# A gated delta layer: token halves of four batches exchanged, triangle solve in opposite corners of the TensorE array, output by channel

## The chip, the cores and the metric

One Trainium2 chip, one of its cores. The metric is the device time of one execution in microseconds (us), the median of several. The kernel is a decoder of 12 sub-layers on 16 batches of 128 tokens and 256 channels, all in float32 at this place; the change touches one sub-layer, the gated delta attention of layer 1 (`layer1_delta`), and two of its constants.

## What is computed

Cut from the reference. Every token has 8 key heads and 16 value heads of 128 channels; `w_qkvz` gives queries, keys, values and the gate z, `w_ba` gives beta and the decay.

```
q, k, v = split(silu(causal_conv4(x @ w_qkvz.T)))
beta = sigmoid(b);  g = -exp(A_log) * softplus(a + dt_bias)
q = q * rsqrt(sum(q * q) + 1e-6);  k = k * rsqrt(sum(k * k) + 1e-6)
def step(S, (qt, kt, vt, gt, bt)):
    S = S * exp(gt)
    delta = (vt - einsum('bhk,bhkv->bhv', kt, S)) * bt
    S = S + einsum('bhk,bhv->bhkv', kt, delta)
    return S, einsum('bhk,bhkv->bhv', qt * 128 ** -0.5, S)
xf = o * silu(z)
xn = xf * rsqrt(mean(xf * xf, -1) + 1e-6) * norm_weight
return xn.reshape(B, T, 16 * 128) @ w_out.T
```

The layer norm of x plus this follows.

## The kernel before

The recurrence over 128 tokens is written as matrices: with A the decayed, beta-weighted, strictly triangular product of keys, the new values are (I + A)^-1 V, and the output is the decayed product of keys and queries times them.

**Rounds.** `layer1_delta` runs 16 rounds. Round i takes key head i // 2 and half of the batches (`batch0(i)`): 8 batches by 2 value heads make 16 slots of 128x128. Everything of a round is in two halves h of 8 slots (`heads(t, h)`); h = 0 is batches 0 to 3, h = 1 batches 4 to 7. Each engine has one function `round_(i)`, an order written out by hand; in it stand the parts of round i, the projections and convolutions of round i + 1 and the gate norm and output projection of round i - 1. Engines meet at semaphores only. PSUM is eight banks, used as four units of two (`unit(n)`).

**TensorE** (`pe`), in order: `turn_values` (L1214, values to token rows), `multiply_keys` (L1220; per batch one product of 256 columns, keys and queries by keys), `project` for round i + 1 (L1200, four units of 1024 columns), `turn_output` of round i - 1 (L1231), `gate_project` (L1208, tokens by channels), `project_out` of i - 1 for h = 0 (L1237), the first triangle product e1 (L1243), `project_out` for h = 1, the sums of squares for the next norm (L1226), three more triangle products (xT1, wT, xT2, L1243: the 64x64 inverses by a Newton step), and the solve. The solve makes the upper 64 rows (`upper`, L1261), takes them across (`across`, L1265), and makes the lower rows (`lower`, L1269), in four quarters of four slots; last the reads, att by solved values (L1388).

**The inverse of the diagonal blocks.** `aT` has 16x16 blocks on its diagonal, 8 for each slot. SyncE sends them to memory, one DMA for each of the 8 block rows with all 16 slots (L1132: 16 partitions by 16 slots by 64 bytes), waits for all, and loads them with one block to each partition (L1134). VectorE inverts all 128 blocks (`invert`, L1672 to L1713, 19 instructions); y and its transpose go to memory (L1136, L1137) and back into `x0` and `xT0`, 8 DMAs each (L1143, L1149). e1 needs `x0`; xT1 needs `xT0` and `p1` (L1767).

**ScalarE** copies projections out (`tap`, L1436 and L1438), does Silu, Exp, Ln, squares and the copies between triangle products; functions of different tables have a table load between them. **VectorE** does normalise (L1633), gate (L1718), the products aT and att with the decay (L1653), the sums over the channels of the squared gated output (L1722) and its scaling (L1726), invert, two decay scans (L1648), convolutions (L1593), the additions to x (L1731), the copies xT2 (L1773) and the additions to the lower values (L1778), and the weighing by beta (L1640). **GpSimd** masks aT to al (L1187).

**Norms through memory.** The key norms are sums over partitions, made by TensorE in four rows. ScalarE takes Ln and Exp, SyncE sends four rows out (`norms_out`, L1105) and one broadcast back to 128 partitions (`norms_in`, L1109). The gate norm is not: it is a VectorE sum over channels, since tokens are on partitions there.

Of the kernel before, what the change touches and what calls it, by code (L numbers as in the profile page):

```python
# [7 lines left out]
F32 = mybir.dt.float32  # L8
# [988 lines left out]
def layer1_delta(nc, g):  # L997
    with Layer(nc, "l1a") as L:
# [4 lines left out]
        outer = L.sb("outer", [128, 128])  # L1003
# [7 lines left out]
        floor = g.mem[:, 8:12, :].rearrange("p a n -> p (a n)")  # L1011
# [3 lines left out]
        e, aT, att, al, vt, z, go, oT, uw = (L.sb(n, [128, VH, 128]) for n in "e aT att al vt z go oT uw".split())  # L1015
# [4 lines left out]
        part = L.sb("part", [128, 64])  # L1020
        x0, xT0, ec, p1, xT1, wT = (L.sb(n, [128, VH, 64]) for n in "x0 xT0 ec p1 xT1 wT".split())
# [4 lines left out]
        ss = L.sb("ss", [128, VH])  # L1026
        rs = L.sb("rs", [128, VH])
# [6 lines left out]
            "z_proj z_out u_made u_out r_made vr_made w_made w_out o_made gated gsq gsum g_ln g_rs g_inverted normed "  # L1034
            "o_turned oT_out out added restored ln_stats ln_mean ln_sqrt ln_out x_turned x_turned_out")
# [11 lines left out]
        def projected(i, u):  # L1047

            return unit(u if i else u % 2)
# [7 lines left out]
        def quarter(n):  # L1057
            return ps[:, 4 + n, :].rearrange("p (k n) -> p k n", n=128)
# [10 lines left out]
        def lows(t, q):  # L1069
            return t[0:64, 4 * q:4 * q + 4, :]  # L1070

        def highs(t, q):
            return t[64:128, 4 * q:4 * q + 4, :]
# [15 lines left out]
        def _(sp):  # L1089
            d = g.dram  # L1090
            for t, name in ((outer, "outer_blocks"), (fold, "fold_ident")):
                sp.dma_start(t[:], d[name]).then_inc(s["rest_loaded"], 16)
            sp.dma_start(floor.rearrange("p (k n) -> p k n", n=S), bc(d["diagonal_floor"], 1, HALF)).then_inc(s["rest_loaded"], 16)
# [16 lines left out]

            norms_out(0)
# [7 lines left out]
            for i in range(ROUNDS):  # L1119
# [46 lines left out]
        def _(pool):  # L1166
# [15 lines left out]
            for i in range(ROUNDS):  # L1182
                for h in range(2):
                    if i:
                        pool.wait_ge(s["r_made"], 4 * i)
# [6 lines left out]
        def _(pe):  # L1192
# [63 lines left out]
            def diagonal(t):  # L1256
                return lambda p0, k: t[p0:p0 + 64, k, p0:p0 + 64]
# [3109 lines left out]
```

## Time and profile before

| what | value |
|---|---|
| runs | 2418.24, 2422.37, 2415.96 us; median 2418.24 |
| profiled execution: span | 2424.5 us (no other time of that execution is given) |
| cores, mean granted TensorE clock | 1, 0.931 |
| TensorE busy | 2112.7 us, 87% of the span |
| VectorE busy | 1856.6 us, 77% |
| ScalarE busy | 1477.2 us, 61% |
| GpSimd busy | 216.2 us, 9% |
| the 16 rounds of the delta layer | about 365 to 1275 us |

Times in the profile are from the first instruction. A float32 product appears as two records, a transpose as one. The duration of a record holds the time through the array; the distance between starts is the rate. Line numbers are those of the kernel printed above.

### The profile page before, as it was taken

What the parts mean: (1) busy time and instruction counts of PE and PEld (TensorE: products, weight loads), DVE (VectorE), ACT (ScalarE), POOL (GpSimd) and SP (SyncE); (2) the same over time, 40 slices, a digit from 0 to 9 for tenths busy, and PEclk for the clock granted to TensorE, in tenths of its full rate; (3) what the DMA queues carried; (4) which work ended last, traced back from release to release, by engine and by line L of the source; (5) the groups of instructions that cost most, each with busy time, mean ns of one, the idle gap of its engine ahead of it and who ended that gap; (6) DMA issues with size and microseconds to landing.
All of it is one profiled execution on the core that took longest, in us unless ns stands there. A gap on an engine that the chain in (4) does not pass through costs nothing. (4 is left out here: it accounts for less than half of the span.)

```text
span 2424.5 us, 42274 instructions
## 1 busy us (share of the span) xinstructions
PE 2112.7 (87%) x16920; PEld 1596.5 (66%) x16920; DVE 1856.6 (77%) x3341; ACT 1477.2 (61%) x2466; POOL 216.2 (9%) x163
## 2 busy tenths in 40 slices
PE   7997447999999999999986589899999996888855
PEld 4666325777777777878774345788888873555633
DVE  4776667888989898889867834478888776678697
ACT  3664255667777777776736631577777775455365
POOL 0000100000100010101100042000000000100313
PEclk8998768999999999999988799999999996999977
DMA  3000012222222221222116355311010000200001
GB/s 159 2 1 12 13 34 53 72 83 57 64 56 66 56 64 54 62 74 80 36 49 212 129 143 176 115 32 57 23 27 6 5 18 1 81 2 1 16 1 35
DMA packets 164785, 135.14 MB, mean 56 GB/s; under 512 B 118512, under 2 KB 145776, under 8 KB 157936
## 3 DMA queue, kind: packets, MB, share of 16 engines
q1 hardware_dynamic: 160752, 126.02, 16.6%
q0 software_dynamic: 3840, 6.43, 1.4%
q8 instruction: 135, 2.21, 0.4%
q14 instruction: 58, 0.48, 0.1%
HBM read 106.42 MB, written 25.98 MB: 55 GB/s over the span
## 5 line engine op out<-in xcount | busy, mean ns | idle before, releaser
L1593 DVE SCALAR_TENSOR_TENSOR ctx_chan<-l1a_raw,l1a_cw,ctx_chan 128x1024 f32<-128x1024 f32 x192 | 232.0, 1279 | 3.5 <-issue 3.5
L1200 PE MATMUL banks<-x_chan,l1a_wp 128*128 128x512 f32 x512 | 225.2, 598 | 4.8 <-ACT l1a_vt L1488 4.8
L1200 PEld LDWEIGHTS banks<-x_chan,l1a_wp 128*128 128x128 f32 x512 | 98.0, 192 | 122.6 <-issue 116.7
L3166 PE MATMUL banks<-x_chan,more_weights_ahead 128*128 128x128 f32 x1024 | 123.6, 275 | 1.2 <-ACT l2a_kT L2693 1.2
L3166 PEld LDWEIGHTS banks<-x_chan,more_weights_ahead 128*128 128x128 f32 x1024 | 121.6, 192 | 3.9 <-ACT l2a_kT L2693 2.0
L1187 POOL TENSOR_TENSOR l1a_al<-l1a_aT,l1a_outer 128x1024 f32<-128x1024 f32 x32 | 75.0, 2364 | 483.2 <-DVE l1a_aT L1653 483.2
L1237 PE MATMUL banks<-l1a_wo,l1a_oT 128*128 128x256 f32 x512 | 117.7, 383 | 0.0
L2706 ACT ACTIVATE l2a_masked<-l2a_masked,l2a_rowmax 128x128 f32<-128x128 f32 x256 | 99.0, 392 | 28.9 <-DVE l2a_rowmax L2919 28.9
L3202 PE MATMUL banks<-l2a_wo,l2a_oT 128*128 128x256 f32 x512 | 114.5, 382 | 0.0
L1208 PE MATMUL banks<-l1a_wz,x_chan 128*128 128x256 f32 x512 | 113.4, 380 | 0.0
L3202 PEld LDWEIGHTS banks<-l2a_wo,l2a_oT 128*128 128x128 f32 x512 | 96.2, 190 | 14.3 <-issue 1.0
L1237 PEld LDWEIGHTS banks<-l1a_wo,l1a_oT 128*128 128x128 f32 x512 | 96.5, 191 | 13.6
L1208 PEld LDWEIGHTS banks<-l1a_wz,x_chan 128*128 128x128 f32 x512 | 96.4, 191 | 12.9 <-issue 0.5
L1436 ACT ACTIVATE l1a_raw<-banks 128x1024 f32<-128x1024 f32 x64 | 65.5, 1024 | 48.8 <-PE banks L1200 48.8
L126 PE MATMUL banks<-ident,x_tok 128*128 128x128 f32 x224 | 43.2, 357 | 40.2 <-ACT x_tok L194 18.4
L3470 ACT ACTIVATE l3a_probsT<-banks 128x512 f32<-128x512 f32 x64 | 38.1, 596 | 59.5 <-PE banks L3636 59.5
L1466 ACT ACTIVATE l1a_oT<-l1a_go 128x1024 f32<-128x1024 f32 x32 | 33.9, 1058 | 64.6 <-DVE l1a_go L1718 64.6
L1778 DVE TENSOR_TENSOR l1a_vt<-banks,l1a_vt 64x512 f32<-64x512 f32 x64 | 44.4, 694 | 37.1 <-PE banks L1265 37.1
L1648 DVE TENSOR_TENSOR_SCAN l1a_e<-ctx_tok 128x1024 f32<-128x1024 f32 x32 | 71.4, 2275 | 1.4 <-DMA ctx_tok<-l1a_rows_mem 1.4
L1438 ACT ACTIVATE ctx_chan<-banks,l1a_cw 128x1024 f32<-128x1024 f32 x64 | 71.0, 1110 | 0.0
L126 PEld LDWEIGHTS banks<-ident,x_tok 128*128 128x128 f32 x224 | 34.3, 185 | 48.7 <-ACT x_tok L194 19.8
L1265 PE MATMUL banks<-l1a_uw,l1a_al 64*64 64x128 f32 x512 | 65.4, 280 | 0.3 <-ACT l1a_uw L1529 0.3
(648 smaller groups left out, 5644.1 us busy)
## 6 DMA issues: line engine op xcount, KB each, us to landing
l1a_sq<-l1a_norm_mem SPq DMA_DIRECT2D x16, 1024.0 KB, 4.7
ctx_tok<-l1a_rows_mem SPq DMA_DIRECT2D x16, 1024.0 KB, 8.1
l1f_wgu<-in_l1f_wgu_dram SPq DMA_DIRECT2D x4, 1408.0 KB, 11.4
moe_sums<-l1x_zero SPq DMA_DIRECT2D x2, 2176.0 KB, 18.3
ctx_chan<-in_ctxT_dram SPq DMA_DIRECT2D x2, 2048.0 KB, 13.8
l1a_wp<-in_l1a_wp_dram SPq DMA_DIRECT2D x8, 512.0 KB, 5.5
l1f_wgu<-moe_sums SPq DMA_DIRECT2D x8, 512.0 KB, 7.5
x_chan<-in_xT_dram SPq DMA_DIRECT2D x4, 512.0 KB, 5.2
```

Of the source, the lines that this page charges most:

```text
L126: mm = nc.tensor.transpose(g.ps[:, n % 2, t * 128:(t + 1) * 128], g.x[:, t0 + t, c * 128:(c + 1) * 128], g.ident[:])
L1187: P.tensor_tensor(heads(al, h), heads(aT, h), bc(outer[:], 1, HALF), ALU.mult).then_inc(s["al_made"], 1)
L1200: mm = MM(projected(i, u)[:, q * 512:(q + 1) * 512], wp[:, c, u * 128:(u + 1) * 128], g.xT[:, c, t0:t0 + 512], start=c == 0, stop=c == 1)
L1208: mm = MM(unit(2 + h)[:, b * 256:(b + 1) * 256], g.xT[:, c, t0:t0 + S], wz[:, c, :], start=c == 0, stop=c == 1)
L1237: mm = MM(unit(h)[:, b * 256:(b + 1) * 256], oT[:, HALF * h + 2 * b + r, :], wo[:, r, :], start=r == 0, stop=r == 1)
L1436: A(raw[:, u, :, CONV - 1:], now, ACT.Copy)
L1438: A(conv[:, u, :], projected(i, u), ACT.Copy, scale=cw[:, c, CONV - 1:]).then_inc(s["tap"], 1)
L1593: V.scalar_tensor_tensor(t, raw[:, u, :, j:j + S], cw[:, c, j:j + 1], t, ALU.mult, ALU.add).then_inc(s["conv_done" if step == 2 else "conv ...
L1648: V.tensor_tensor_scan(heads(e, h).rearrange("p k n -> p (k n)"), rows[:, h * 1024:(h + 1) * 1024], floor, 0.0, ALU.add, ALU.max).then_inc ...
L2706: ins = A(probs[:, k, :], masked[:, k, :], ACT.Exp, bias=rowmax[:, k:k + 1], scale=128 ** -0.5, accum_out=rsum[:, k:k + 1])
L3166: mm = mm_(ps[:, 4 + q % 2, k * 128:(k + 1) * 128], wq[:, c, SHARE * q + k, :], g.xT[:, c, tile(i)], start=c == 0, stop=c == 1)
L3202: mm = mm_(ps[:, 6, 0:D], oT[:, h, :], wo[:, h, :], start=h == 0, stop=h == HEADS - 1)
```

## The change

Half h = 1 (batches 4 to 7) keeps its two 64-token halves exchanged: in `e`, `aT`, `att`, `al` and the values, tokens 0 to 63 stand on partitions 64 to 127 and the rest on 0 to 63. Beta is turned accordingly, the scan has a floor of its own for each half, the mask `outer` too. The solve then works for the two halves in opposite corners of the array at the same time: `early` and `late` values have tiles of their own, all 8 slots of both halves go through each step in two groups of four, and the copies in between take 128 partitions. Keys are multiplied in products of 64 rows by 128 columns (the quarter that is zero is left out) with one increment for both halves. The reads come out by channel, with the two token parts accumulated: early for all tokens, late for the last 64. So the gate is projected by channel, the output transposes and their copies go, `go` is the stationary operand of the output projection, and the gate norm becomes a sum over partitions on TensorE which goes through memory (`widths_through`). Both output projections stand behind e1. The blocks are sent in 16 DMAs. Ln of the next norm moves behind the `wT` copies. One scan moves ahead of the inversion.

```diff
+            def widths_through(i):
+                sp.wait_ge(s["g_rs"], i + 1)
+                for j in range(4):
+                    sp.dma_start(width_mem[j:j + 1, :], widths[32 * j:32 * j + 1, :]).then_inc(s["width_out"], 16)
+                sp.wait_ge(s["width_out"], 64 * i + 64)
+                sp.dma_start(gsq[:].rearrange("p k n -> p (k n)"), width_mem.rearrange("j n -> (j n)").partition_broadcast(128)).then_inc(s["width_in"], 16)
...
-                sp.wait_ge(s["a_made"], 2 * i + 2)
...
-                for b in range(8):
-                    here = slice(BLK * b, BLK * b + BLK)
-                    sp.dma_start(blk_mem[b].rearrange("h r c -> r h c"), aT[here, :, here]).then_inc(s["blk_out"], 16)
-                sp.wait_ge(s["blk_out"], 128 * i + 128)
+                for h in range(2):
+                    sp.wait_ge(s["a_made"], 2 * i + h + 1)
+                    for b in range(8):
+                        here, turn = slice(BLK * b, BLK * b + BLK), (BLK * b + 64 * h) % 128
+                        sp.dma_start(blk_mem[b, HALF * h:HALF * h + HALF].rearrange("h r c -> r h c"),
+                                     aT[here, HALF * h:HALF * h + HALF, turn:turn + BLK]).then_inc(s["blk_out"], 16)
+                sp.wait_ge(s["blk_out"], 256 * i + 256)
                 sp.dma_start(blk[:, 0:BLK * BLK], blk_mem.rearrange("b h r c -> (b h) (r c)")).then_inc(s["blk_in"], 16)
+                if i:
+                    widths_through(i - 1)
...
+            def keys_by(h, b, rows, s0, t0):
+                at = (4 * h + b) * S
+                out = unit(2 + h)[rows, b * 256:(b + 1) * 256].rearrange("p (w n) -> p w n", w=2)[:, :, t0:t0 + 64]
+                return MM(out, conv[:, 0, at + s0:at + s0 + 64], conv[:, 0:2, at + t0:at + t0 + 64], start=True, stop=True)
...
+                for b in range(4):
+                    for t0 in (0, 64):
+                        for h in range(2):
+                            keys_by(h, b, first_rows(h), 0, t0)
+                    keys_by(1, b, second_rows(1), 64, 64)
+                    mm = keys_by(0, b, second_rows(0), 64, 64)
                 mm.then_inc(s["products"], 1)
...
+            def sum_gated():
+                for j in range(4):
+                    mm = MM(ps[32 * j:32 * j + 32, 4, :], g.ones[:, 0:32], gsq[:, 4 * j:4 * j + 4, :], start=True, stop=True)
+                mm.then_inc(s["gsum"], 1)
...
+            def upper(h, k):
+                at = first_rows(h)
+                return MM(pairs(1, k // 4)[at, k % 4, :], xT2[at, HALF * h + k, :], early[at, k, :], start=True, stop=True)
+            def across(h, k):
+                at = first_rows(h)
+                return MM(pairs(0, k // 4)[second_rows(h), k % 4, :], al[at, HALF * h + k, 64:128], solved_early[at, k, :], start=True, stop=True)
+            def read_early(h, k):
+                at = first_rows(h)
+                return MM(slots(2 + h)[:, by_channel(h, k), :], solved_early[at, k, :], att[at, HALF * h + k, :], start=k < 2, stop=False)
+            def read_late(h, k):
+                at = second_rows(h)
+                return MM(slots(2 + h)[:, by_channel(h, k), 64:128], solved_late[at, k, :], att[at, HALF * h + k, 64:128], start=False, stop=k >= HALF - 2)
...
             def solve(i):
+                pe.wait_ge(s["xT2_out"], 2 * i + 2)
+                for c in range(2):
+                    each(upper, c).then_inc(s["u_made"], 1)
+                if i:
+                    pe.wait_ge(s["added"], 2 * i)
+                for c in range(2):
+                    pe.wait_ge(s["u_out"], 2 * i + c + 1)
+                    each(across, c).then_inc(s["r_made"], 1)
+                if i + 1 < ROUNDS:
+                    pe.wait_ge(s["norm_ln"], i + 2)
+                for c in range(2):
+                    each(read_early, c)
+                for c in range(2):
+                    pe.wait_ge(s["vr_made"], 2 * i + c + 1)
+                    each(lower, c).then_inc(s["w_made"], 1)
+                for c in range(2):
+                    pe.wait_ge(s["w_out"], 2 * i + c + 1)
+                    mm = each(read_late, c)
+                mm.then_inc(s["o_made"], 1)
```

ScalarE's and VectorE's orders, cut to the moved parts (ScalarE first):

```diff
+                    A(early[first_rows(h), :, :], slots(h)[0:64], ACT.Silu)
+                    A(late[second_rows(h), :, :], slots(h)[64:128], ACT.Silu).then_inc(s["v_out"], 1)
...
+                if i:
+                    width_ln(i - 1)
+                    width_rs(i - 1)
...
-                    norm_ln(i + 1)
...
                 if more:
+                    norm_ln(i + 1)
                     norm_rs(i + 1)
...
                 for h in range(2):
                     take_products(i, h, att, 1).then_inc(s["att_made"], 1)
-                if i:
-                    for h in range(2):
-                        scale_gated(i - 1, h)
+                if more:
+                    scan(i + 1, 0)
                 invert(i)
+                if i:
+                    v.wait_ge(s["width_in"], 16 * i)
+                    for h in range(2):
+                        V.tensor_tensor(heads(go, h), heads(go, h), heads(gsq, h), ALU.mult).then_inc(s["normed"], 1)
                 if more:
-                    for h in range(2):
-                        scan(i + 1, h)
+                    scan(i + 1, 1)
```

## Rows read from the trace of the kernel before

**Rows 1.** The page, its first line.

```profile
span 2424.5 us, 42274 instructions
```

**Rows 2.** Busy time by stretch: us, then busy us (instructions) of each engine, clock, DMA share, GB/s.

```profile
430.00:1210.00 780.00, 777.26 (x7577) 609.37 (x7576) 692.74 (x792) 553.57 (x636) 77.65 (x35) 1.00 0.22 62
```

**Rows 3.** Timeline of TensorE, one round: start, us, engine, line, operation, out<-in, xcount.

```profile
706.55 3.84 PE L1388 MATMUL banks<-l1a_uw,l1a_att 128*128 128x128 f32 x32
710.22 1.91 PE L1214 MATMUL banks<-ident,ctx_chan 128*128 128x128 f32 x16
711.97 3.62 PE L1220 MATMUL banks<-ctx_chan 128*128 128x256 f32 x16
715.42 13.90 PE L1200 MATMUL banks<-x_chan,l1a_wp 128*128 128x512 f32 x32
729.16 1.91 PE L1231 MATMUL banks<-ident,l1a_go 128*128 128x128 f32 x16
730.90 7.07 PE L1208 MATMUL banks<-l1a_wz,x_chan 128*128 128x256 f32 x32
737.81 3.62 PE L1237 MATMUL banks<-l1a_wo,l1a_oT 128*128 128x256 f32 x16
741.36 2.08 PE L1243 MATMUL banks<-l1a_x,l1a_al 64*64 64x64 f32 x64
743.37 3.72 PE L1237 MATMUL banks<-l1a_wo,l1a_oT 128*128 128x256 f32 x16
747.65 1.06 PE L1226 MATMUL banks<-l1a_sq,ones 128*32 128x512 f32 x8 [0.56 <-ACT l1a_sq L1448]
...
754.41 1.96 PE L1261 MATMUL banks<-l1a_vt,l1a_p 64*64 64x128 f32 x16
...
760.08 1.96 PE L1269 MATMUL banks<-l1a_vt,l1a_p 64*64 64x128 f32 x16
761.97 3.28 PE L1388 MATMUL banks<-l1a_uw,l1a_att 128*128 128x128 f32 x27
```

**Rows 4.** Timeline of VectorE in that round.

```profile
710.17 2.36 DVE L1718 TENSOR_TENSOR l1a_go<-banks,l1a_z 128x1024 f32<-128x1024 f32 x2
...
725.33 0.18 DVE L1672 COPY l1a_y<-l1a_blk 128x8 f32<-128x8 f32 x1 [1.70 <-DMA l1a_blk<-l1a_blk_mem]
...
732.12 4.46 DVE L1648 TENSOR_TENSOR_SCAN l1a_e<-ctx_tok 128x1024 f32<-128x1024 f32 x2
736.50 9.63 DVE L1593 SCALAR_TENSOR_TENSOR ctx_chan<-l1a_raw,l1a_cw,ctx_chan 128x1024 f32<-128x1024 f32 x8
...
747.18 1.21 DVE L1767 TENSOR_TENSOR l1a_p<-l1a_ec,l1a_fold 128x1024 f32<-128x1024 f32 x1
```

**Rows 5.** Timeline of ScalarE in that round.

```profile
753.34 1.28 ACT L1462 ACT_TABLE_LOAD   x1
754.64 0.63 ACT L1462 ACTIVATE l1a_lengths<-l1a_lengths 128x512 f32<-128x512 f32 x1
```

**Rows 6.** Timeline of SyncE's queue, and one line of the page's DMA issues.

```profile
716.88 3.77 SPq L1132 DMA_DIRECT2D l1a_blk_mem<-l1a_aT  x8
723.33 0.34 SPq L1134 DMA_DIRECT2D l1a_blk<-l1a_blk_mem  x1
...
733.97 3.75 SPq L1143 DMA_DIRECT2D l1a_x<-l1a_yT_mem  x8
...
757.32 0.34 SPq L1109 DMA_DIRECT2D l1a_sq<-l1a_norm_mem  x1
...
2062.66 0.43 SPq L3438 DMA_DIRECT2D ctx_chan<-l3x_keys_ahead  x1
2063.14 0.44 SPq L3439 DMA_DIRECT2D ctx_tok<-l3x_vals_ahead  x1
...
l1a_sq<-l1a_norm_mem SPq DMA_DIRECT2D x16, 1024.0 KB, 4.7
```

**Rows 7.** Last round: a stretch of the table, and TensorE's timeline.

```profile
1217.00:1221.00 4.00, 3.27 (x16) 3.28 (x17) 3.56 (x12) 1.03 (x1) 0.00 (x0) 0.50 0.13 37
...
1217.73 3.67 PE L1231 MATMUL banks<-ident,l1a_go 128*128 128x128 f32 x16 [6.96 <-DVE l1a_go L1726]
```

**Rows 8.** Timeline of TensorE in the first layer: tiles of 32 rows.

```profile
106.45 1.17 PE L516 MATMUL banks<-l0a_kT,l0a_qT 32*128 32x128 f32 x32
```

More of the change, by code:

```diff
@@ L1014, in layer1_delta @@
         lengths = L.sb("lengths", [128, 512])
-        e, aT, att, al, vt, z, go, oT, uw = (L.sb(n, [128, VH, 128]) for n in "e aT att al vt z go oT uw".split())
+        e, aT, att, al, z, go, gsq = (L.sb(n, [128, VH, 128]) for n in "e aT att al z go gsq".split())
+        early, late, solved_early, solved_late = (L.sb(n, [128, HALF, 128]) for n in "early late solved_early solved_late".split())
         blk = L.sb("blk", [128, PITCH])
@@ new lines, in each @@
+            def each(product, c):
+                for k in range(4 * c, 4 * c + 4):
+                    for h in range(2):
+                        mm = product(h, k)
+                return mm
+            def solve(i):
+                pe.wait_ge(s["xT2_out"], 2 * i + 2)
+                for c in range(2):
[16 more added lines that the diff above has]
+                mm.then_inc(s["o_made"], 1)
@@ L1316, in round_ @@
+                multiply_keys()
                 if more:
@@ L1373, in round_ @@
                 for h in range(2):
-                    slot_half(6, h, within(p1), within(xT0)).then_inc(s["xT1_made"], 1)
+                    slot_half(2, h, within(p1), within(xT0)).then_inc(s["xT1_made"], 1)
+                if i and more:
+                    pe.wait_ge(s["squared"], i + 2)
+                    pe.wait_ge(s["added"], 2 * i - 1)
+                    sum_squares()
                 for h in range(2):
@@ L1380, in round_ @@
                     pe.wait_ge(s["wT_out"], 2 * i + h + 1)
-                    slot_half(6, h, within(ec), within(wT)).then_inc(s["xT2_made"], 1)
+                    slot_half(2, h, within(ec), within(wT)).then_inc(s["xT2_made"], 1)
                 if i == 0:
-                    next_sums()
+                    pe.wait_ge(s["squared"], 2)
+                    sum_squares()
                 solve(i)
-                for h in range(2):
-                    pe.wait_ge(s["w_out"], 4 * i + 2 * h + 2)
-                    for k in range(HALF * h, HALF * h + HALF):
-                        mm = MM(slots(2 + h)[:, k % HALF, :], att[:, k, :], uw[:, k, :], start=True, stop=True)
-                    mm.then_inc(s["o_made"], 1)
             for c in range(DC):
@@ L1494, in round_ @@
                         tap(i + 1, u)
+                if i:
+                    width_ln(i - 1)
+                    width_rs(i - 1)
+                if more:
                     for u in range(2, 4):
                         tap(i + 1, u)
-                if i:
-                    for h in range(2):
-                        output_turned(i - 1, h)
-                if more:
                     for h in range(2):
```

313 lines of the change are left out of this document (128 added, 185 removed).

## The prediction

> **What bounds the kernel now.** The page first: one core, span 2424.5 us [rows 1]. That is 6.3 us above the median of the three runs (2418.24); the sum below is a difference inside the profiled execution and is then laid on the median. Only the delta layer changes. The table of stretches shows that in its 14 full rounds TensorE is busy for 777.26 of 780 us at a granted clock of 1.00 [rows 2]. The same read starts at 706.55 and 761.97 [rows 3]: a round takes 55.42 us. The timeline of TensorE [rows 3] is one unbroken list; those of VectorE, ScalarE and SyncE [rows 4 to 6] show what runs beside it. So TensorE's work bounds the round. What the reader is to see next is how little slack the chain beside it has. From the value transposes at 710.22, which I call zero: both halves of `aT` are made when SyncE starts the eight DMAs of the diagonal blocks, at 6.66; it waits, and issues the load back at 13.11; the inversion starts at 15.11; the eight `x0` loads start at 23.75, take about 3.3 us to the last one's start and, at the 2.0 us that the block load needed from issue to use, are in at 29.05 [rows 4, 6]. The first triangle product starts at 31.14 [rows 3]. The slack is 2.1 us.
>
> **TensorE's list.** Each number is a distance between starts in rows 3. The output transposes go (729.16 to 730.90: 1.74). The keys took 3.45; they become 24 products of 128 columns, 48 records, in two column halves. The nearest rate is that of two 64-wide tiles at once: the 5.67 us from 754.41 to 760.08 hold 16 lone records (at the rate of the last 16, 1.89) and 64 paired ones, so 0.060 each, 2.9 in all. Sums of the gated squares come in: 1.0, as the sums at 747.65. Gate and output projections keep their columns. The solve was 5.67 + 1.89 + 3.67 = 11.23; now it is five passes of 32 paired records, 160 x 0.060 = 9.6, and 0.3 of waits for copies. In pure work that is -1.74 - 0.55 + 1.0 - 1.3, about 2.6 us less a round.
>
> No row has a float32 product on 64 rows and 128 columns. Bounds for the 64 records of the two reads: 32-row tiles of that width ran 32 records in 1.17 us, 0.036 each [rows 8]; one tile at a time costs the 0.115 of the old read. I take 0.060, nearer to the first because those are also row tiles with 128 columns; the ends are -1.5 and +3.5 us a round. For the keys the upper end is likewise 0.115 a record, +2.7.
>
> Changes of tile shape rise from 5 to 13 a round. At 741.36 and 743.37 [rows 3] the next shape starts 0.07 us before the modelled end of the last record, where equal shapes, as at 711.97, overlap by 0.16: a change costs about 0.1. Three or four are on the new path; I take 0.3. The Trainium skill, TensorEngine Tiling (Array Packing), Key Properties, says that changing the tiling mode drains TensorE. A full drain would be some 0.2 a change and speaks against this change of the kernel; the trace shows the smaller price.
>
> **New waits.** (a) `o_made` now comes once, after the last read, so both gates start behind it (at 710.17 they overlapped it [rows 4]). The norm of the next keys is later too. Its Ln no longer runs ahead of the triangle products but after the `wT` copies, before the Exp: the Exp with its table load takes 1.94 [rows 5], and I count the Ln the same. The trip through memory stays: 2.05 from the Exp's end to the second issue and 4.7 to landing [rows 5, 6], 6.7. Counting back from the next zero: the copies end at -12.0 (9.9 solve, 1.0 wait below, and the rest of the last triangle product), Ln and Exp at -8.1, the norms are in at -1.4, two normalises and two gates at 2.36 a pair [rows 4] end at 3.3. TensorE's transposes are done at 1.75, so it stands 1.5 us, and the keys run from 3.3 to 6.2. (b) All keys carry one increment; `aT` is made from 6.4, its first half at 7.65, the second at 8.8. (c) `blk_out` becomes 16 DMAs of half the size. SyncE's eight take 3.77 us, 0.49 from start to start, with 256 pieces each by the code; two loads of 128 partitions, at 2062.66 and 2063.14, are 0.48 apart [rows 6]. The price hangs on the DMA, not on its pieces. The bounds are 0.25 (half) and 0.49; I take 0.49. The last one starts at 15.0 and ends at 15.45; the old wait from there (720.65 to 723.33, 2.68) gives 18.1 for the load back, 20.1 for the inversion. Behind that wait on SyncE's queue stand the five `width` DMAs, `yT`, `x0` and `xT0`; on VectorE's, behind the blocks, stand the scaling, one scan and the convolutions. (d) `x0` starts 8.64 after the inversion, as before: 28.75, in at 34.05.
>
> TensorE has nothing to do from 27.8 (6.2 + 13.74 projections + 1.0 sums + 6.9 gate projections) to 34.1: it idles 6.3 us. Then 2.0 for the triangle product, 2 x 3.55 output (one half used to come before it), 6.76 sums and triangle products as from 747.65 to 754.41, 1.0 because the solve now needs both halves of `xT2` (its 0.69 copy and handoffs, hidden before), 9.9 solve. The round ends at 60.9 against 55.4: **+5.4 us** after rounding.
>
> (e) The clock. An idle stretch of 6.96 us before 1217.73 left the granted clock at 0.50 over 1217 to 1221 [rows 7], that is 1.2 instead of 2.4 GHz. The new idle stretch is as long. Four to five us at half speed lose 2.0 to 2.5; I take **2.2 us**. The bound below is nothing, if the clock stays.
>
> Costed at nothing: the value Silu in four parts (about +1.9 on ScalarE; the first pair ends at 3.1, needed at 6.2); width Ln and Exp over 512 (TensorE's third projection covers the Ln until 17.5); the width trip: Exp done at 19.1, then the same 6.7, in at 25.8, covered by the inversion until 27.0. If the blocks came early that cover is gone, and this trip is next in line. VectorE loses two reductions and two additions (some 3.7 us), but it then waits for blocks from 13.1 to 20.1. After the inversion it needs 2.35 scaling, 2.2 scan, 9.6 convolution and 1.2 for `p1` [rows 4]: 42.3, one us before TensorE needs it. VectorE is thus the next bound behind the blocks.
>
> **Sum.** 5.4 + 2.2 + 0.3 = 7.9 us a round. The 14 full rounds and the last (whose block chain grows alike) make 15: 118.5 us. 2418.24 + 118.5 = about **2537 us** (2543 for the span). The first round I leave out: its own convolutions and norms are late already.
>
> **Rivals.**
> 1. *The clock stays or the DMAs are cheaper.* Without the half clock: 5.7 x 15 = 86, 2504 us. With DMAs at 0.25 the blocks come 3.6 us earlier and no long idle is left, but then the width trip decides: 25.8, scaling 28.1, scan 30.4, Exp 31.4, a table load 32.7, Silu of z 34.7, and only then the output projections. That round is 59.4: 2418 + 60 = 2478. For it: the pieces are halved. Against it: the equal spacing in rows 6. Together 0.30.
> 2. *TensorE's list stays the bound, and it is faster.* This decides if `x0` is in by 27.8, 6.3 us before my walk; the place is SyncE's queue at the blocks. It needs 16 issues in about 1.6 us, or the wait of 2.68 to shrink as well. Then a round is 60.9 - 6.3 = 54.6, 0.8 less, 15 x 0.8 = 12: 2406 us; without the gate wait 2383. For it: TensorE is busy 99.6% today [rows 2] and loses 2.6 us of work. Against: every gap above. 0.13.
> 3. *Tiles don't pair.* If the row tiles of the solve don't run together, the reads alone cost 3.5 us more: 2537 + 52 = 2589. For it: no row shows the shape. Against: the products at 741.36, whose row halves write one bank, run 64 records in 2.01 us. 0.07. The page named above, Gotcha 1, says that different row tiles cannot access one PSUM bank at the same time; by it the new solve would be serial, and the row at 741.36 speaks against that.
> 4. *Gains and waits cancel,* within 0.3%: 0.04.
>
> The forecast, slower with the clock falling, has the remaining 0.46.
>
> **How the numbers follow.** About 0.3% is what a measurement of this kernel can tell from no change. Faster by more: 0.13 (rival 2). Within: 0.04. Slower: 0.46 + 0.30 + 0.07 = 0.83. The range runs from 2465, below rival 1's lower end, to 2590, rival 3; what it leaves out is rivals 2 and 4 and a little.
>
> **What would show it.** Right: a round of about 63 us; SyncE's 16 block DMAs 0.49 apart, over 7.5 us; TensorE idle some 6 us before the first triangle product, waiting for `x0`; the granted clock near 0.5 behind that gap; an idle of 1.5 us ahead of the keys and 1.0 ahead of the solve; five passes of the solve of 1.9 each. Wrong: block DMAs under 0.4 apart, no idle before the first triangle product, a clock of 1.00 throughout, or read passes of 3.7 us.

## The result and the profile after

The changed kernel takes 2526.02 us in the median of four runs (2522.88 to 2528.57); the kernel before, beside it, took 2417.1 us (2415.71 to 2422.37). The ratio is 1.0438, with a 95% interval of [1.0419, 1.0457]: slower by 4.4%. The profiled execution has a span of 2526.7 us against 2424.5 [rows 1].

The page's first line, then the table of stretches of the kernel after: the stretch of [rows 2], and the 14 full rounds (all but the first and the last).

```profile
span 2526.7 us, 43534 instructions
430.00:1210.00 780.00, 691.46 (x7118) 478.84 (x7120) 593.16 (x665) 478.86 (x519) 65.66 (x32) 0.95 0.24 73
427.41:1292.49 865.08, 765.60 (x8067) 534.45 (x8065) 653.23 (x730) 527.74 (x575) 71.24 (x35) 0.95 0.24 73
```

Where [rows 2] had TensorE busy for 777.26 of 780 us, it is now busy for 691.46, at a mean clock of 0.95 instead of 1.00. The full rounds take 865.08 / 14 = 61.79 us each; before they took 55.02 (from the transposes at 435.1 to those at 1205.4 us). That is 6.77 us a round.

TensorE in the round that starts at 735.70 us (line numbers are those of the new kernel; the idle time stands in brackets at the end):

```profile
756.68 7.03 PE L1230 MATMUL banks<-x_chan,l1a_wz 128*128 128x512 f32 x16
769.23 3.68 PE L1279 MATMUL banks<-l1a_x,l1a_al 64*64 64x64 f32 x64 [5.52 <-DMA l1a_x<-l1a_yT_mem]
772.83 7.27 PE L1273 MATMUL banks<-l1a_wo,l1a_go 128*128 128x256 f32 x32
...
787.79 1.96 PE L1302 MATMUL banks<-l1a_early,l1a_p 64*64 64x128 f32 x32 [0.80 <-DVE l1a_p L1797]
790.34 1.96 PE L1306 MATMUL banks<-l1a_solved_early,l1a_al 64*64 64x128 f32 x32 [0.59 <-ACT l1a_solved_early L1557]
792.24 2.06 PE L1314 MATMUL banks<-l1a_att,l1a_solved_early 64*128 64x128 f32 x32
794.22 1.96 PE L1310 MATMUL banks<-l1a_late,l1a_p 64*64 64x128 f32 x32
796.12 2.00 PE L1318 MATMUL banks<-l1a_att,l1a_solved_late 64*128 64x64 f32 x32
798.05 1.96 PE L1235 MATMUL banks<-ident,ctx_chan 128*128 128x128 f32 x16
801.41 2.84 PE L1241 MATMUL banks<-ctx_chan 128*64 128x128 f32 x48 [1.40 <-DVE l1a_go L1749]
```

The list of [rows 3] has one hole of 0.56 us; here there are four. The largest stands before the first triangle product (`e1`, the one that reads `x0`), and that product takes 3.68 us instead of the 2.08 of [rows 3]. The table of stretches shows why, in the clock column (the third from the end):

```profile
764.00:769.20 5.20, 0.00 (x0) 0.00 (x0) 5.20 (x5) 2.72 (x3) 0.00 (x0) 0.71 0.30 28
769.20:773.00 3.80, 3.77 (x65) 3.66 (x66) 3.80 (x4) 2.15 (x3) 0.00 (x0) 0.50 0.33 31
773.00:780.00 7.00, 7.00 (x32) 5.92 (x32) 7.00 (x7) 4.30 (x5) 0.00 (x0) 1.00 0.01 2
```

TensorE idles, the granted clock falls within the idle time (0.71 in the mean of it) to 0.50, that is 1.2 instead of 2.4 GHz, and it is back at 1.00 when the output projections are under way. SyncE's queue in the same round, and VectorE's first instruction of the inversion. (The sixteen block DMAs of this round hold one gap of 1.92 us; in most rounds they take 7.44 us in all.)

```profile
743.11 8.89 SPq L1151 DMA_DIRECT2D l1a_blk_mem<-l1a_aT  x16
753.11 0.34 SPq L1154 DMA_DIRECT2D l1a_blk<-l1a_blk_mem  x1
754.82 1.11 SPq L1125 DMA_DIRECT2D l1a_width_mem<-ctx_tok  x4
756.84 0.34 SPq L1127 DMA_DIRECT2D l1a_gsq<-l1a_width_mem  x1
761.98 0.34 SPq L1158 DMA_DIRECT2D l1a_yT_mem<-l1a_yT  x1
...
764.10 3.77 SPq L1165 DMA_DIRECT2D l1a_x<-l1a_yT_mem  x8
```

```profile
755.10 0.17 DVE L1703 COPY l1a_y<-l1a_blk 128x8 f32<-128x8 f32 x1 [5.08 <-DMA l1a_blk<-l1a_blk_mem]
```

The last view gives every round at once: TensorE's groups over the 14 full rounds (busy us, mean ns | idle us before them and what ended it).

```profile
L1273 PE MATMUL banks<-l1a_wo,l1a_go 128*128 128x256 f32 x448 | 109.0, 404 | 0.4 <-ACT l1a_z L1510 0.4
...
L1279 PE MATMUL banks<-l1a_x,l1a_al 64*64 64x64 f32 x896 | 47.0, 294 | 59.3 <-DMA l1a_x<-l1a_yT_mem 59.3
L1241 PE MATMUL banks<-ctx_chan 128*64 128x128 f32 x672 | 43.1, 288 | 20.3 <-DVE l1a_go L1749 20.3
...
L1302 PE MATMUL banks<-l1a_early,l1a_p 64*64 64x128 f32 x448 | 27.5, 272 | 11.2 <-DVE l1a_p L1797 11.2
L1306 PE MATMUL banks<-l1a_solved_early,l1a_al 64*64 64x128 f32 x448 | 27.5, 271 | 8.3 <-ACT l1a_solved_early L1557 8.3
```

Divided by 14, the idle time is 4.24 us before `e1`, 1.45 before the keys, 0.80 and 0.59 in the solve: 7.08 us a round, where before there was 0.2.

Two things meet before `e1`. In the mean of the 14 rounds, counted from the value transposes, `x0` has landed at 32.7 us instead of 28.3, so its chain is 4.3 us longer. And TensorE is ready for `e1` at 28.5 instead of 31.1, since output transposes and one output projection no longer stand in front of it: the work that covered the chain has shrunk by 2.6 us.

Outside the full rounds: the first is 63.66 us instead of 69.62; the last, from its transposes to the end of its reads, is 60.2 (1292.49 to 1352.69) instead of 50.9; from there to the next layer's first tile 34.5 instead of 27.4.

### The profile page after: what moved, and what is told of

Its sections match the earlier page's. It is cut to its first block and busy times, and to the rows that moved or that the text cites. A ratio compares the mean times of both kernels' runs of the same rounds, so it can differ in the third digit from the quotient of the medians.

```text
span 2526.7 us, 43534 instructions
## 1 busy us (share of the span) xinstructions
PE 2098.8 (83%) x17509; PEld 1512.0 (60%) x17560; DVE 1817.2 (72%) x3278; ACT 1459.0 (58%) x2407; POOL 210.7 (8%) x163
## 5 line engine op out<-in xcount | busy, mean ns | idle before, releaser
L1273 PE MATMUL banks<-l1a_wo,l1a_go 128*128 128x256 f32 x512 | 125.8, 407 | 5.2 <-DVE l1a_go L1847 4.8
L1273 PEld LDWEIGHTS banks<-l1a_wo,l1a_go 128*128 128x128 f32 x512 | 104.3, 207 | 23.3 <-DVE l1a_go L1847 5.8
L1279 PE MATMUL banks<-l1a_x,l1a_al 64*64 64x64 f32 x1024 | 52.8, 290 | 74.1 <-DMA l1a_x<-l1a_yT_mem 74.1
L1230 PE MATMUL banks<-x_chan,l1a_wz 128*128 128x512 f32 x256 | 113.4, 596 | 0.0
L1279 PEld LDWEIGHTS banks<-l1a_x,l1a_al 64*64 64x64 f32 x1024 | 49.8, 200 | 87.3 <-DMA l1a_x<-l1a_yT_mem 87.3
L1480 ACT ACTIVATE l1a_e<-l1a_e 128x1024 f32<-128x1024 f32 x32 | 33.7, 1056 | 102.3 <-DVE l1a_e L1679 102.3
L1230 PEld LDWEIGHTS banks<-x_chan,l1a_wz 128*128 128x128 f32 x256 | 48.9, 192 | 62.9 <-issue 62.9
L126 PE MATMUL banks<-ident,x_tok 128*128 128x128 f32 x224 | 43.4, 359 | 40.5 <-ACT x_tok L194 18.1
L1684 DVE TENSOR_TENSOR l1a_aT<-banks,l1a_e 128x1024 f32<-128x1024 f32 x32 | 37.7, 1219 | 49.5 <-issue 49.5
L3487 ACT ACTIVATE l3a_probsT<-banks 128x512 f32<-128x512 f32 x64 | 38.1, 596 | 59.4 <-PE banks L3653 59.4
L1800 DVE TENSOR_TENSOR l1a_late<-banks,l1a_late 128x512 f32<-128x512 f32 x32 | 22.1, 691 | 66.5 <-PE banks L1306 66.5
## 6 DMA issues: line engine op xcount, KB each, us to landing
ctx_chan<-in_ctxT_dram SPq DMA_DIRECT2D x2, 2048.0 KB, 13.7
```

The costliest lines, as they stand in the source:

```text
L126: mm = nc.tensor.transpose(g.ps[:, n % 2, t * 128:(t + 1) * 128], g.x[:, t0 + t, c * 128:(c + 1) * 128], g.ident[:])
L1230: mm = MM(unit(h)[:, r * 512:(r + 1) * 512], wz[:, c, r * 128:(r + 1) * 128], g.xT[:, c, t0:t0 + 512], start=c == 0, stop=c == 1)
L1273: mm = MM(unit(n)[:, b * 256:(b + 1) * 256], go[:, HALF * h + 4 * r + b, :], wo[:, r, :], start=r == 0, stop=r == 1)
L1279: return MM(ps[p0:p0 + 64, bank + k // HALF, k % HALF * 64:(k % HALF + 1) * 64], lhsT(p0, k), rhs(p0, k), start=True, stop=True)
```

## Experiments

The profile leaves two readings of the 4.24 us: the chain of the blocks alone, or that chain and a second one beside it that would end at the same moment. Each kernel was timed four times (the last one six times) beside the kernel before; ratios are to it. Marks in the code cuts: `...` stands for lines or arguments left out.

### The price of sixteen block DMAs, in the kernel before

```diff
-sp.wait_ge(s["a_made"], 2 * i + 2)
...
-for b in range(8):
-    sp.dma_start(blk_mem[b]..., aT[here, :, here])
+for h in range(2):
+    sp.wait_ge(s["a_made"], 2 * i + h + 1)
+    for b in range(8):
+        sp.dma_start(blk_mem[b, HALF * h:HALF * h + HALF]..., aT[here, HALF * h:HALF * h + HALF, here])
```

> The kernel before, with only its eight block DMAs replaced by sixteen half-sized ones, the first eight of them allowed to start when the first half of aT stands, as in the changed kernel. Theory (the number of block DMAs sets when x0 arrives, 0.49 us each on SyncE): the first eight start about 2.3 us earlier, sixteen take 7.8 us instead of 3.9, so blocks, inversion and x0 come about 1.6 to 2 us later in each round, about 2447 us in all. Rival A (blocks are not what binds, other work of the round covers them): 2418 us, no change. Rival B (half-sized DMAs are issued faster, so sixteen cost as much as eight): 2418 us or a little less, with sixteen issues in 4 us in the trace.

2447.44 us, ratio 1.0117 [1.0087, 1.0147]; full rounds of 56.36 us against 55.02. SyncE's queue, then TensorE's groups that wait:

```profile
715.35 7.68 SPq L1133 DMA_DIRECT2D l1a_blk_mem<-l1a_aT  x16
...
L1245 PE MATMUL banks<-l1a_x,l1a_al 64*64 64x64 f32 x896 | 29.1, 219 | 8.9 <-ACT l1a_z L1482 8.4 <-issue 0.3
L1228 PE MATMUL banks<-l1a_sq,ones 128*32 128x512 f32 x112 | 14.9, 605 | 10.3 <-ACT l1a_sq L1450 10.3
```

Half-sized DMAs are issued 0.47 us apart (the round shown has one gap of 0.79) and full-sized ones 0.49, so rival B falls, and the total is what the theory said. Its path is not: the new idle time waits for z and for the squares, and not for `x0`, which lands at 30.1 us of the round while `e1` starts at 31.9 (means). That z and the squares are late because the inversion on VectorE is 2 us later is read from the order of the work and was not tested.

### Blocks and widths, one at a time and together

Eight DMAs instead of sixteen in the changed kernel, or the widths' way back left out, or both. The first kernel leaves out the diagonal blocks of the second half (it sends other columns in their place), the second leaves out the scaling by the widths (it multiplies by what stands in the tile); neither computes the layer's values, but the engines' instructions stay the same:

```diff
-for h in range(2):
-    sp.wait_ge(s["a_made"], 2 * i + h + 1)
-    for b in range(8):
-        sp.dma_start(blk_mem[b, HALF * h:...], aT[here, HALF * h:..., turn:turn + BLK])
+sp.wait_ge(s["a_made"], 2 * i + 2)
+for b in range(8):
+    sp.dma_start(blk_mem[b]..., aT[here, :, here])
```

```diff
-sp.wait_ge(s["width_out"], 64 * i + 64)
-sp.dma_start(gsq[:]..., width_mem...partition_broadcast(128))
...
-v.wait_ge(s["width_in"], 16 * i)
+v.wait_ge(s["gsum"], i)
```

> The changed kernel with eight block DMAs of all sixteen slots each, all at the columns of the first half (so the diagonal blocks of the second half's slots are taken from other columns, and the values are not the reference's; every shape, wait and size stays). Theory: x0 comes about 2.4 to 2.8 us earlier per round, the idle time before the e1 products falls from 5.5 us to about 2.5 to 3, and with it some of the slow clock goes; the trip of the widths through DRAM, or the gates' outputs z, then decide the start of the output projections. Round 59.0 to 59.6 us instead of 61.8, total 2482 to 2492. Rival (the wait for x0 only stands in front of another one of the same length, the widths'): less than 1 us per round, over 2510.

> The changed kernel without the way back of the widths: they still go out to DRAM, but the transfer that spreads them over the partitions and every wait for it are left out, and VectorE multiplies by the old squares in their place (so the values are not the reference's, every instruction on the engines stays). All sixteen block DMAs stay. Theory (two chains of equal length end before the output products, the one over x0 and the one over the widths, VectorE's scan and z; removing one leaves the other): x0 still comes at 32.5 us of the round, less than 1 us gained, 2510 to 2526. Rival (the widths' transfer is what delays both, the x0 chain too): 3 us or more per round, below 2485.

> The changed kernel with both edits: eight block DMAs (second half's blocks at wrong columns) and no way back of the widths. Theory (two chains of equal length, both shortened now): VectorE's scaling starts at 22.7 us of the round instead of 26.0, z ends at about 31.7 instead of 34.9, x0 is in at about 30, and the output products start at 32 instead of 35.8: 3.5 to 4 us less per round, 2465 to 2478. Rival (something else sets the length of a round, as x0 alone did not): less than 1.5 us per round, over 2503.

The last three columns are means over the 14 full rounds, in us from the value transposes: when the last `x0` DMA has landed, when the last Silu of z ends, when the first output projection starts.

| | ratio, interval | median us | full round | `x0` in | z done | output starts |
|---|---|---|---|---|---|---|
| changed kernel | 1.0438 [1.0419, 1.0457] | 2526.0 | 61.79 | 32.7 | 35.2 | 36.1 |
| eight block DMAs | 1.0440 [1.0401, 1.0479] | 2522.7 | 61.44 | 32.1 | 35.4 | 35.6 |
| no widths back | 1.0396 [1.0353, 1.0440] | 2515.9 | 61.38 | 32.4 | 34.2 | 35.6 |
| both | 1.0201 [1.0169, 1.0234] | 2468.0 | 57.72 | 30.1 | 31.8 | 32.5 |

Each edit alone brings 0.4 us a round, which the intervals don't tell from nothing; both bring 4.1. TensorE's `e1` group in the three, in this order:

```profile
L1277 PE MATMUL banks<-l1a_x,l1a_al 64*64 64x64 f32 x896 | 45.6, 288 | 56.0 <-DMA l1a_x<-l1a_yT_mem 56.0
```

```profile
L1278 PE MATMUL banks<-l1a_x,l1a_al 64*64 64x64 f32 x896 | 46.0, 290 | 55.5 <-DMA l1a_x<-l1a_yT_mem 55.5
```

```profile
L1276 PE MATMUL banks<-l1a_x,l1a_al 64*64 64x64 f32 x896 | 34.3, 241 | 23.7 <-DMA l1a_x<-l1a_yT_mem 23.7
```

My expectation for the first was wrong, and the rival's number (over 2510) held: the blocks did come 2.7 us earlier (inversion at 15.9 us of the round in the mean, instead of 18.6), and still `x0` came only 0.6 earlier. The other two came out as expected. SyncE's queue in a round of that kernel, and its page's row of `yT`:

```profile
755.67 0.34 SPq L1127 DMA_DIRECT2D l1a_gsq<-l1a_width_mem  x1
757.93 0.34 SPq L1156 DMA_DIRECT2D l1a_yT_mem<-l1a_yT  x1
...
761.40 3.77 SPq L1163 DMA_DIRECT2D l1a_x<-l1a_yT_mem  x8
...
l1a_yT_mem<-l1a_yT SPq DMA_DIRECT2D x16, 128.0 KB, 4.2
```

The transfer that spreads the widths (1 MB) is issued 2.3 us before `yT`, which then needs 4.2 us to land in the median; in the changed kernel it is 1.7, and there the widths have landed or nearly so (issued at 756.84, median 4.6) when `yT` goes out at 761.98. So the two chains are tied twice over: the scaling and z wait for the widths, and `yT`, which `x0` is read from, lands late while the widths' transfer is under way. That is shown by the pair: with eight DMAs and no widths, `yT` is back at 1.7 and the idle time before `e1` falls to 1.7 us a round. What these two don't give back is open: the round of 57.72 is still 2.7 us longer than before the change.

### Is the slow clock the idle time's doing?

Extra matmuls into a bank that nobody reads, between gate projection and `e1`; twenty, then five:

```diff
+if i and more:
+    pe.wait_ge(s["tap"], 4 * i + 7)
+    for _ in range(20):
+        MM(ps[:, 7, :], wz[:, 0, 0:128], g.xT[:, 0, 0:512], start=True, stop=True)
 pe.wait_ge(s["x0_in"], 128 * i + 128)
```

> The changed kernel with twenty extra matmuls of 512 columns (into a PSUM bank that nobody reads) in the gap between the gate projection and the e1 products, so that TensorE is busy there. Theory (the half clock at e1 and at the first output products comes from the idle 5.5 us before them): the granted clock stays at full, e1 takes 2.08 us instead of 3.68, 1.6 us less per round, about 2502 us. Rival A (the slow clock comes from the whole round's activity, or the time lost there is given back before the next wait): within 5 us of 2526. Rival B (the extra matmuls run late and hold e1 up): slower than 2526.

It took 2681.37 us, ratio 1.1077 [1.1045, 1.1108]: rival B, by my own mistake about the size. One float32 matmul of 512 columns is two records of 0.433 us, so twenty take 17.3 us. The clock part of the theory held all the same: `e1` took 2.08 us in every full round. With five:

> As the run with twenty extra matmuls, but with five: one of them took 0.87 us there (two records of 0.433), so five take 4.3 us and fit in the gap of 4.3 us before the e1 products. Theory (the idle gap costs the clock, and the clock costs 1.3 us in e1 and 0.6 in the output products; z then holds the output products up from 34.9 on): the granted clock of the rounds is full, 1.2 to 1.5 us less per round, 2505 to 2510. Rival (a gap that short costs no clock, the slow stretch has another reason): clock as before and 2526 or more.

2510.6 us, ratio 1.0365 [1.0330, 1.0399], 0.6 us above the range of the theory; full rounds of 60.27 us (1.5 less).

```profile
L1273 PE MATMUL banks<-l1a_wo,l1a_go 128*128 128x256 f32 x448 | 100.4, 382 | 4.0 <-ACT l1a_z L1514 4.0
...
L1279 PE MATMUL banks<-l1a_x,l1a_al 64*64 64x64 f32 x896 | 29.1, 220 | 2.9 <-DMA l1a_x<-l1a_yT_mem 2.9
```

Against the changed kernel `e1` drops from 47.0 to 29.1 us and the output projections from 109.0 to 100.4: 1.28 and 0.61 us a round, the price of the clock. Work that computes nothing makes the kernel faster. What then waits is z (4.0), the second chain.

### Pairs of opposite corners

```diff
-for k in range(4 * c, 4 * c + 4):
-    for h in range(2):
+for h in range(2):
+    for k in range(4 * c, 4 * c + 4):
         mm = product(h, k)
```

> The changed kernel with the tiles of the solve issued as four of one corner and then four of the opposite corner, instead of one of each in turn: the same tiles, the same values, other neighbours. Theory (neighbours in opposite corners of the array run together, and that alone brings 32 records in 1.96 us): each of the five groups of 32 takes about 3.7 us instead of 2.0, 8 to 9 us more per round, 2640 to 2665 us. Rival (the array takes the tiles at their rate in any order, or evictions set the pace of the solve): under 2 us per round, below 2556.

2550.37 us, ratio 1.0543 [1.0510, 1.0577]; full rounds of 63.15 us. The rival's numbers held (below 2556, under 2 us a round), its reason only in part. One group of the solve, over the full rounds:

```profile
L1302 PE MATMUL banks<-l1a_early,l1a_p 64*64 64x128 f32 x448 | 35.9, 275 | 11.2 <-DVE l1a_p L1797 11.2
```

35.9 / 14 = 2.56 us for 32 records instead of 1.96. The order matters, but four products of one corner and then four of the other still overlap for the most part: 0.080 a record, between the 0.061 in turn and the 0.118 of one corner alone (16 records in the 1.89 us from 760.08 to 761.97 [rows 3]). TensorE is busy 2.9 us longer a round; the full rounds grow by only 1.4, as it waits 1.5 less, 0.8 of it before the keys.

### Reordering what binds

If the two chains are tied, moving both must pay. Four of the sixteen block DMAs go to ScalarE's queue, the widths come before the second tap, and the scan that z waits for before the scaling:

```diff
-    for b in range(8):
+    for b in range(8 - 4 * h):
         sp.dma_start(blk_mem[b, HALF * h:...], aT[here, HALF * h:..., turn:turn + BLK])
...
-for u in range(2):
-    tap(i + 1, u)
+tap(i + 1, 0)
+act.wait_ge(s["a_made"], 2 * i + 2)
+for b in range(4, 8):
+    act.dma_start(blk_mem[b, HALF:VH]..., aT[here, HALF:VH, turn:turn + BLK])
 width_ln(i - 1)
 width_rs(i - 1)
+tap(i + 1, 1)
...
 invert(i)
+scan(i + 1, 1)
 (scaling by the widths)
-scan(i + 1, 1)
```

> The changed kernel with three reorderings that keep its values: four of the sixteen block DMAs go out on ScalarE's queue after its first tap, ScalarE makes the widths before its second tap, and VectorE does the scan's second half (which z waits for) before the scaling. Theory (both chains shortened together): blocks about 2 us earlier, widths about 1 us earlier, z done at about 31 to 32 us of the round, x0 in at about 30.5 to 31.5, output products from about 33 on: 2.5 to 3.5 us less per round, 2475 to 2492. Rival (the transfer of the widths runs at the same time as yT's and holds x0 up as it did with eight block DMAs): less than 1 us per round, over 2510.

2475.78 us, ratio 1.0226 [1.0190, 1.0262], as expected: full rounds of 58.10 us, the idle time before `e1` 28.3 us in 14 rounds. The same values as the changed kernel, 2% faster. Then the keys' wait by itself, in the changed kernel:

```diff
-sp.dma_start(sq[:]..., norm_mem...partition_broadcast(128)).then_inc(s["norm_in"], 16)
+for u in range(2):
+    sp.dma_start(sq[:, u, :], norm_mem[2 * u:2 * u + 2, :]...partition_broadcast(128)).then_inc(s[("norm_in", "norm_in2")[u]], 16)
...
-v.wait_ge(s["norm_in"], 16 * i + 16)
+v.wait_ge(s[("norm_in", "norm_in2")[u]], 16 * i + 16)
```

> The changed kernel with the norms of the squares brought back by two transfers of half the size, one for each of the two normalisations, instead of one that both wait for; values unchanged. Theory (TensorE's 1.3 us before the key products is VectorE's list after the wait for the norms: two normalisations, then two gate multiplications that must be done before the banks are free; an earlier first normalisation takes that list's idle 1.2 us away): the key products start at 2.2 to 2.5 us of the round instead of 3.2, 0.7 to 1.1 us less per round, 2510 to 2517. Rival (two transfers share the queue and both land when the single one did, or x0 keeps its distance to the start of the round): within 4 us of 2526.

2524.47 us, ratio 1.0447 [1.0426, 1.0469]: the rival. The wait before the keys stayed at 20.7 us in 14 rounds. Half-sized transfers landed after 5.0 us in the median, the single one after 4.7. Next, the three reorderings, the norms in halves, and three of the eight `x0` DMAs on ScalarE's queue as well:

```diff
-for b in range(8):
+for b in range(5):
     sp.dma_start(x0[here, :, cols], yT_mem[b]...)
...
 decay_exp(i + 1, 0)
+act.wait_ge(s["yT_out"], 16 * i + 16)
...
+for b in range(5, 8):
+    act.dma_start(x0[here, :, cols], yT_mem[b]...)
 decay_exp(i + 1, 1)
```

> The kernel with the three reorderings (four block DMAs on ScalarE's queue, widths before the second tap, scan before the scaling) plus the norms in halves plus three of the eight x0 DMAs on ScalarE's queue, issued between its two decay exponentials. Theory (the way of x0 is issue after issue at 0.47 to 0.49 us; fewer in a row bring it earlier): x0 comes about 1.4 us earlier, e1 starts at 28.5 to 29.3 of the round, z ends at 31 to 31.5 and then decides, and the key products start about 1 us earlier: 2 to 2.5 us less per round than with the three reorderings alone, 2440 to 2450. Rival (ScalarE's queue costs as much as it saves, z moves back by what x0 gains): 2465 or more.

2458.21 us, ratio 1.0161 [1.0142, 1.0180], full rounds of 57.10: better than the reordering alone, between what I expected (2440 to 2450) and the rival (2465 or more). TensorE's waiting groups:

```profile
L1242 PE MATMUL banks<-ctx_chan 128*64 128x128 f32 x672 | 45.9, 299 | 21.1 <-DVE l1a_go L1765 21.1
L1280 PE MATMUL banks<-l1a_x,l1a_al 64*64 64x64 f32 x896 | 29.1, 220 | 10.2 <-DMA l1a_x<-l1a_yT_mem 10.2
...
L1303 PE MATMUL banks<-l1a_early,l1a_p 64*64 64x128 f32 x448 | 27.5, 272 | 18.1 <-DVE l1a_p L1814 18.1
```

`x0` costs 0.7 us a round now, and the clock stays at full for `e1` (29.1). But the wait before the solve grew from 0.80 to 1.29: in the round looked at VectorE has no pause from the inversion to the `xT2` additions, and the wait ends with these. Covering it with the last batch of the output projection (and moving VectorE's addition of that half behind the `xT2` additions), and the tail's gaps with extra matmuls:

```diff
-project_out((3, 0)[h], h)
+project_out((3, 0)[h], h, range(4 - h))
...
 slot_half(2, h, within(ec), within(wT))
+project_out(0, 1, range(3, 4))
...
-add(i - 1, 1)
 (the xT2 additions)
+add(i - 1, 1)
...
+for _ in range(n):
+    MM(ps[:, bank, :], wz[:, 0, 0:128], g.xT[:, 0, 0:512], start=True, stop=True)
```

> The kernel with the seven DMAs on ScalarE's queue and the norms in halves, and two more edits: the output projection's last batch of the second half (two of sixteen products) is issued after the xT2 products, with VectorE's addition after its xT2 additions, where TensorE waits 0.8 us; and extra matmuls into unread banks in the last round's and the tail's gaps. Theory (the wait before the upper solve is the time of VectorE's additions and can be covered; the tail pays the slow clock for its gaps): 0.7 to 0.8 us less per round and 4 to 8 us once, 2422 to 2436. Rival A (VectorE's later addition holds the across products up instead): no gain per round, 2436 to 2446. Rival B: the tail's gaps cost nothing by their clock, 2430 to 2440.

2454.17 us, ratio 1.0136 [1.0102, 1.0170]: above all three ranges, with full rounds of 57.32, not shorter.

```profile
L1281 PE MATMUL banks<-l1a_xT,l1a_p 64*64 64x64 f32 x896 | 29.1, 220 | 17.6 <-DVE l1a_p L1815 17.6
```

The wait before the upper solve is gone from the list, and 1.26 us a round stand before the xT1 products in its place, where they wait for VectorE's `p1`: the batch that moved had covered it. The tail: broad sums and output projection in the changed kernel, then the broad sums in this one:

```profile
1355.55 5.37 PE L1267 MATMUL banks<-l1a_gsq,ones 128*128 128x512 f32 x8 [2.86 <-ACT l1a_gsq L1496]
1365.75 9.45 PE L1273 MATMUL banks<-l1a_wo,l1a_go 128*128 128x256 f32 x32 [4.83 <-DVE l1a_go L1847]
```

```profile
1288.04 3.70 PE L1268 MATMUL banks<-l1a_gsq,ones 128*128 128x512 f32 x8
```

The sums are 1.7 us shorter with TensorE kept busy, and from the last round's transposes to the end of the span it is 1226.3 us instead of 1230.4 in the kernel of the run before: the 4 us at the low end of what was expected. Last, in the kernel with seven DMAs on ScalarE's queue and the tail's extra matmuls, but without the moved batch, the loads that SyncE issued right behind the norms wait until the norms have been used:

```diff
 for i in range(ROUNDS):
+    sp.wait_ge(s["kq_normed"], 2 * i + 2)
...
 norms_in(i + 1)
+sp.wait_ge(s["kq_normed"], 2 * i + 4)
```

> The kernel with seven DMAs on ScalarE's queue and the norms in halves, plus the tail's extra matmuls (without the moved output batch), and SyncE now waits for the two normalisations before it issues the loads of the rows, wp, wo and wz, which until here it issued within 1.5 us behind the norms' transfers. Theory (the norms' transfers take 4.8 us whole or in halves because the loads behind them share the DMA engines; that sharing is also what makes one round in three longer, by the wait before the key products): each half lands 1 to 2 us earlier, the key products' wait falls to its floor of 0.75 us in nearly all rounds, the mean round falls from 57.1 to 56.0 to 56.3 us, total 2436 to 2446. Rival A (the transfers' time is their own, latency and broadcast reads): landing times stay at 4.8 us and the time at 2450 to 2458. Rival B (the later rows or wp now hold up the scan or the projections): over 2458.

2442.18 us, ratio 1.0086 [1.0070, 1.0102].

```profile
L1244 PE MATMUL banks<-ctx_chan 128*64 128x128 f32 x672 | 39.8, 274 | 15.2 <-DVE l1a_go L1775 15.2
```

The total and the rounds (56.36) are the theory's, the mechanism is not the one I wrote: the norms' median landing stayed at 4.8 us. What shrank is the worst case, from 7.7 us with the seven DMAs moved to 6.1, and with it the long rounds: there four of fourteen took 58.3 to 60.1 us, here the longest takes 57.1. The keys also run without slow clock (39.8 us against 45.9). Against that kernel the 14 rounds give 10.3 us, and what lies behind them 7.6, where the extra matmuls stand. Why the longest landings became shorter was not tested further.

This is the fastest of the changed kernels here: 3.4% less than the changed kernel (1.0086 against 1.0438), yet still 0.9% more than the kernel before. None beat that.

## Why the prediction was right, and where it was off

Forecast 2537 us, measured 2526; the sign, the bound and the chain were right. By the terms:

- **TensorE's work.** Said: about 2.6 us less a round, with 0.3 of waits in the solve counted in; so 2.9 less of pure work and 0.3 back for changes of shape, -2.6. Measured: the last kernel runs the same list at full clock in 736.49 us per 14 rounds, 52.61 each, against 54.84 before: -2.2. The reads pair (2.06 and 2.00 us for 32 records), as taken; the keys take 2.84, where 2.9 was said.
- **The chain of `x0`.** Said in the round's time, and measured in the round from 735.70: load back 18.1 and 17.4; inversion 20.1 and 19.4; `x0` issued 28.75 and 28.4; in at 34.05, `e1` at 33.5. In the mean of 14 rounds it is earlier: load back 16.7, inversion 18.6, `x0` issued 27.5, `e1` at 32.7. The sixteen issues ended where they were said to (15.5 against 15.45). What was too long is the wait behind them, from the last issue to the load back: 2.68 was taken from one round of the kernel before, but 11 of its 16 rounds have 1.25 and only 3 have 2.7; in the changed kernel it is 1.1 in every round. TensorE also comes free a little later than said, at 28.5 and not 27.8. So the idle time was 6.3 in the forecast and 4.24 in the mean.
- **Other waits.** Keys 1.5, measured 1.45; solve 1.0 and 0.3, measured 0.80 and 0.59.
- **The clock.** Said 2.2 us; TensorE's busy time is 54.69 a round against 52.61 at full clock, 2.1.
- **The round.** 7.08 idle, +2.1 clock, -2.2 work, -0.2 idle before: 6.8 us, where I had 7.9. The mis-sized term is the idle time before `e1`, by 2. Two smaller errors point the other way and hide half of it: the work falls by 0.4 less than said, and the round that I started from was a long one, 55.42 with 0.56 of idle time, where the mean is 55.02 with 0.2.

The sum "7.9 x 15 = 118.5" is near the measured 108.9 partly by luck. The spans of the profiled executions differ by 102.2 (the one of before was 6 above its median). Of that the 14 full rounds give 94.8; the last round, which I took as one more of the same, and the tail, which I left out, give 9.3 + 7.1 = 16.4 instead of 7.9; the first round and what lies ahead of it give back 7.7, which I left out too, and what lies behind the tail gives back 1.3. In the last round TensorE idles 13.7 us before `e1`, because there is no next projection to fill it, and the tail's norm (squares, broad sums, two table loads, Ln, Exp) is longer than the reductions it replaces. I costed neither. Why the first round is 6.0 us shorter was not tried.

Rival 1 had the width trip "next in line", with a round of 59.4 when the blocks come early. The mechanism was right and its margin wrong. I counted the trip in at 25.8, covered until 27.0. In the mean it lands at 26.2 with the inversion done at 25.5: there is no cover left. I also missed that `yT` lands 2.5 us later while that transfer is under way. With eight block DMAs the round was 61.4 and not 59.4: output starts at 35.6 instead of 34.7, and the idle time before `e1`, which rival 1 took to be gone, stays at 4.0 us and keeps its slow clock. That VectorE is "the next bound behind the blocks" showed once both chains were moved.

The Trainium skill, TensorEngine Tiling (Array Packing), Key Properties, says that changing the tiling mode drains TensorE. Here the products that follow a change start 0.06 us before the modelled end of the last record (794.22 + 1.96 against 796.12), where equal shapes overlap by 0.16, so this trace too shows a price of 0.1. No run shows the full drain that the prediction puts at 0.2. The same page of the Trainium skill, Gotcha 1: PSUM Pressure, says that different row tiles cannot access the same PSUM bank simultaneously. By it the new solve would be serial; this trace does not agree, as the upper solve's two row tiles write one bank and its 32 records take 1.96 us, where one corner alone needs 0.118 a record.

## What to carry to other kernels

When a change takes work from the engine that is full, ask which chain has the least slack beside it and count its DMA issues one by one: here half the size took 0.47 us an issue instead of 0.49. Ask also what work leaves the stretch that covered that chain. When shortening one chain brings nothing, try the next one together with it before giving up the theory; two edits of 0.4 us a round were worth 4.1 as a pair. Price an idle gap with the clock: here a gap of 4 us cost another 2 behind it. And take a wait from more than one round: one round's 2.68 was 1.25 in most others.

## What the runs showed of the hardware

- SyncE issues the block DMAs 0.49 us apart at 16 KB (8 in 3.77 us) and 0.47 apart at 8 KB (16 in 7.44 us in 8 of the 14 rounds of the changed kernel). In the others one gap among the sixteen is longer, up to 1.9 us; why was not tested. It is not the price of every DMA: the four DMAs of the widths, one row each, are 0.28 us apart (1.11 us for four).
- A DMA of 128 KB lands after 1.7 us in the median, and after 4.2 when it is issued 2.3 us behind a 1 MB transfer on the same queue. Halving a broadcast of 1 MB left its landing time at 4.8 to 5.0 us (4.7 as a whole).
- Tiles of opposite corners overlap even when four products of one corner precede four of the other: 0.080 us a record, 0.061 in strict turn, 0.118 for one corner alone.
- Matmuls whose results nobody reads kept the granted clock at full and made the kernel 0.7% faster (1.0365 against 1.0438).
